# Layer 2's weight maxima first, its quantisation over 37 heads, and layer 1's maxima beside it through one raw buffer

## The chip, the cores and the metric

The kernel runs on one core of one Trainium2 chip. The metric is the device time of one launch in microseconds (us), the median of several runs. A core has five engines with their own instruction streams: TensorE (PE, matmul; its weight loads are listed apart as PEld), VectorE (DVE), ScalarE (ACT), GpSimd (POOL) and SyncE (SP), which here issues every DMA in one queue. They are tied by semaphores alone; nothing reorders the streams.

## The reference, cut to what matters

```python
x = x + tanh(g_xattn[0]) * L0_xattn_ref(ctx_2048, ctx_2048, layernorm(x), ssm_kernel, D, 8)   # x: (8, 512, 1024)
x = x + tanh(g_ffn[0]) * L0_ffn_ref(layernorm(x), ln_w, ln_b, W1, b1, W2, b2)

# the mixer, for each of 64 heads of 8 channels, over length L = 1024
kv = einsum('bhil,bhjl->bijhl', k, v)                  # here k = v, so kv is symmetric in i, j
y = irfft(rfft(kv, 2 * L) * rfft(ssm_kernel, 2 * L))[..., :L]
out = einsum('bijhl,bhil->bjhl', y + kv * D, q)

# the MLP: 1024 -> 4096 -> 1024, every operand in shared-exponent int8 blocks of 32
def mx_quant(x):
    amax = max(abs(x)) over blocks of 32
    scale = exp2(floor(log2(amax)) - 6)
    return clip(round(x / scale), -128, 127) * scale
h = mx_linear(mx_layernorm(x), W1, b1); h = mx_gelu(h); h = mx_linear(h, W2, b2)
```

## The kernel before, in words

The program has two stages. The first, `mixer_block`, does the convolution as matmuls with a Toeplitz slab of the taps, head by head, 64 heads in all. The second, `ffn_block`, does the MLP. Both weight matrices have to be quantised, which needs the maximum of each block of 32, and DVE does much of this beside the convolution, where PE is the busy engine.

A head `h` on PE is 78 matmuls in five stretches (L304 to L322). Its first stretch waits for `lo_ready`, the low half of the products kk of this head, which DVE makes at L495 in the head before. Its third stretch waits for `products_ready`, that is for DVE to have read the second half of the last head's result out of `y_ps`. In odd heads PE also transposes: `turn_back` (L343) after the first stretch and `turn_q` after the third.

DVE's order in head `h` is written out at L666 to L700. It starts when PE has finished head `h-1`:

1. `times_q(h-1, 1)`: L509, L512, L515 read the second half of the last head's result.
2. `make_kk(h+1)`: L486, L489. ACT then copies k, squares it and makes `kk_hi` (L395).
3. In even heads `ln_stats`, in odd heads `residual` (L658).
4. `times_q(h, 0)`, which waits for PE's second stretch of head `h`.
5. `low_half(h+1)`: L495, which waits for `kk_hi` and releases PE's head `h+1`.
6. What the texts below call the **filler** of head `h`: work for the MLP. It runs ahead of `times_q(h, 1)` in DVE's stream, so what of it is not done when PE starts head `h+1` delays step 1 of head `h+1`. That overhang is called the **carry** into head `h+1`.

The filler before the change: heads 0 to 19 hold 13 of the 32 tiles of weight maxima (L615, 1 MB each), and heads 3 to 20 also the norm and quantisation of the first input tiles. Heads 21 to 33 hold the other 19 maxima, two in each odd head and one in each even head except head 33. Head 34 makes all the scales (`weight_scales`, L640 to L648). Heads 35 to 63 hold layer 2's quantisation: 16 tiles of three instructions each, `layer2_ints` (L624), `layer2_clip` (L629), `layer2_quant` (L634). The maxima come through three raw buffers in `arena`, so that a load is issued two or three maxima ahead of its use.

SP's order in head `h` (L260 to L288): wait until PE has finished head `h-1` and issue two slab loads for head `h+1`; wait for `kk_ready` and `squares_ready` and load k for head `h+3`; in odd heads wait for `x1_ready`, store the x1 tile (L238) and load an x tile (L197); then loads of raw weights (L214 for maxima, L221 for quantisation) and stores of quantised ones (L226).

After the scales, layer 1's inverse scales are spread to all partitions in four steps at `spread_heads` (36, 38, 40, 42): ACT `repeat_inverses` (L421), PE `spread_inverses` (eight matmuls in the head's second stretch), ACT `keep_inverses` (L429). `turn_back` of the next odd head writes the same PSUM tile, so it waits for `inv_kept`. ACT's stream has `ln_apply` (L409, L413), which waits for POOL's `inv_sqrt` (L735), ahead of `keep_inverses`. POOL sums the products of each head (L748 to L760).

Of the kernel before, what the change touches and what calls it, by code (L numbers as in the profile page):

```python
# [20 lines left out]
L = 1024  # L21
HID = 4096
# [48 lines left out]
def mixer_block(nc, x_t, ctx_e, taps_in, skip_in, g_x, scratch, x1_t, w_m, w2_t, w2_q, ln_w, ln_b, arena, w_inv, rs, shift1,  # L71
# [10 lines left out]
    heads = tiles * TILE_HEADS  # L82
    row = LB * PAIR
    early_heads = 4 * EARLY
    maxima_heads = list(range(6)) + list(range(7, early_heads + 5, 2))
    maxima_heads += [early_heads + 5 + 2 * n // 3 for n in range(2 * W_TILES - len(maxima_heads))]
    maxima_of = [[n for n in range(2 * W_TILES) if maxima_heads[n] == h] for h in range(heads)]
    scales_head = maxima_heads[-1] + 1
    maxima_slot = [n % 2 if n < 12 else (n - 12) % 3 for n in range(2 * W_TILES)]
    spread_heads = [scales_head + 2 + scales_head % 2 + 2 * i for i in range(4)]  # L90
    w2_heads = heads - scales_head - 1
    ints_of, clip_of, quant_of = [{scales_head + 1 + (3 * j + i) * w2_heads // (3 * W_TILES): j for j in range(W_TILES)}
                                  for i in range(3)]
    y_base = -PARTS[0][0] * PAIR % 512
    edges = [0] + list(range(512 - y_base, row, 512)) + [row]
# [1 line left out]
    with ExitStack() as stack:  # L97
        def sb(name, shape, dt):
            return stack.enter_context(nc.sbuf_tensor(name, shape, dt))
# [4 lines left out]
        def sem(name):  # L104
            return stack.enter_context(nc.semaphore(name))
# [29 lines left out]
        w2_scale = w_max[:, 0:L // 2].bitcast(BF16)  # L135
        inv_rows = w_max[:, L:L + L // 2].bitcast(BF16)
        inv_T = raw_weights(arena, 1).bitcast(BF16)
        w_raw = w2_raw = [raw_weights(arena, i) for i in (2, 3, 0)]
        x1_last = raw_weights(arena, 2)[:, L:2 * L]
        w2_int = arena[:, X_LOADS * L:(X_LOADS + 1) * L].bitcast(I16)  # L140
        ident_bf = sb("ident_bf", [P, P], BF16)
# [21 lines left out]
        w_loaded = [sem(f"w_m_loaded{i}") for i in range(3)]  # L163
        w_max_ready, w_floor, w_bits, w_inv_ready = sem("w_max_ready"), sem("w_floor"), sem("w_bits"), sem("w_inv_ready")
# [26 lines left out]
        def _(sp):  # L191
# [15 lines left out]
            def load_w(n):  # L207
                slot = maxima_slot[n]
                users = [m for m in range(n) if maxima_slot[m] == slot]
                if users:  # L210
                    sp.wait_ge(w_max_ready, users[-1] + 1)
                elif slot == 2:
                    sp.wait_ge(e_input, EARLY)
                sp.dma_start(w_raw[slot], w_m[n]).then_inc(w_loaded[slot], 16)  # L214

            def load_w2(j):
                if j < 3:
                    sp.wait_ge(w_max_ready, 2 * W_TILES)
# [34 lines left out]
            load_k(2)  # L253
            for t in range(2, X_SLOTS):
                load_x(t)
            load_w(0)
            load_w(1)
            for dst, src in ((lnw_b, ln_w), (lnb_b, ln_b)):
                sp.dma_start(dst, bass.AP(tensor=src.tensor, offset=0, ap=[[0, P], [1, L]])).then_inc(ln_loaded, 16)
            for h in range(heads):  # L260
                t = h // TILE_HEADS
                if 1 <= h < heads - 1:
                    sp.wait_ge(y_ready, 2 * h)
                    load_slab(h + 1)
                if h + 3 < heads:
                    sp.wait_ge(kk_ready, h + 2)
                    sp.wait_ge(squares_ready, h + 2)
                    load_k(h + 3)
                if h % TILE_HEADS == 1 and t >= 1:
# [5 lines left out]
                if h == early_heads + 4:  # L275
                    load_w(14)
                for n in maxima_of[h - 1] if h >= 1 else []:
                    for m in range(n + 1, 2 * W_TILES):
                        if maxima_slot[m] == maxima_slot[n]:
                            load_w(m)  # L280
                            break
# [91 lines left out]
        def _(act):  # L373
# [41 lines left out]
                                     scale=rstd[:]).then_inc(xn_ready, 1)  # L415

            def repeat_inverses(r):
                act.wait_ge(w_inv_ready, 2)
                if r >= 1:
                    act.wait_ge(inv_spread, r)  # L420
                nc.scalar.copy(inv_rows.rearrange("p (n r k) -> p n r k", r=P // QB, k=QB),  # L421
                               view(w_inv, r * LB * QB, [(QB, LB), (0, P // QB), (1, QB)])).then_inc(inv_repeated, 1)

            def keep_inverses(r):
                if r == 0:
                    for turned in e_turned:
                        act.wait_ge(turned, 16 * EARLY // 2)
# [37 lines left out]
        def _(dve):  # L465
# [146 lines left out]
            def weight_maxima(n):  # L612
                nb = HID // 2 // QB
                dve.wait_ge(w_loaded[maxima_slot[n]], 16 * maxima_slot[:n + 1].count(maxima_slot[n]))
                nc.vector.tensor_reduce(w_max[:, n * nb:(n + 1) * nb], w_raw[maxima_slot[n]].rearrange("p (k i) -> p k i", k=nb),  # L615
                                        AX.X, ALU.max, apply_absolute_value=True).then_inc(w_max_ready, 1)

            def layer2_ints(j):
                dve.wait_ge(w2_loaded[j % 3], 16 * (j // 3 + 1))
                if j == 0:  # L620
                    dve.wait_ge(w_inv_ready, 2)
# [16 lines left out]
            def weight_scales():  # L638
                dve.wait_ge(w_max_ready, 2 * W_TILES)
                nc.vector.tensor_scalar(w_max[:], w_max[:], TINY, None, ALU.max).then_inc(w_floor, 1)  # L640
                dve.wait_ge(w_floor, 1)
                upper_half = w_max[:].bitcast(U16).rearrange("p (n two) -> p n two", two=2)[:, :, 1]
                nc.vector.tensor_scalar(w_inv.bitcast(U16), upper_half, EXP_BITS, EXP_BITS,
                                        ALU.bitwise_and, ALU.bitwise_xor).then_inc(w_bits, 1)
                dve.wait_ge(w_bits, 1)
                nc.vector.tensor_scalar(w_inv, w_inv, float(QB), None, ALU.mult).then_inc(w_inv_ready, 1)
                dve.wait_ge(w_inv_ready, 1)
                nc.vector.tensor_scalar(w2_scale.bitcast(U16), w_inv[:, L:2 * L].bitcast(U16), -1.0, 254.0 * 128,  # L648
                                        ALU.mult, ALU.add).then_inc(w_inv_ready, 1)

            def residual(t):
                dve.wait_ge(back_ready, t + 1)
# [13 lines left out]
            for h in range(heads):  # L666
# [700 lines left out]
```

## Time and profile before

| what | value |
|---|---|
| median of 3 runs | 1983.67 us (1983.58, 1983.67, 1988.19) |
| the profiled execution's own time | 1986.38 us |
| its span, first to last instruction | 1984.5 us |
| PE busy | 1899.7 us, 96% |
| DVE busy | 1694.7 us, 85% |
| POOL busy | 956.1 us, 48%; all of it in the first half |
| ACT busy | 755.0 us, 38% |
| the convolution on PE | its first matmul waits 17.7 us for the slab; it ends near 1019 us; 64 heads |
| mean granted PE clock | 0.984 of full speed |

An engine's busy share is a mean over stages. In the convolution the question is whether PE goes without a gap; where it does, time that DVE, ACT, POOL or a DMA spends costs nothing. In a timeline row a bracket at the end holds the engine's idle time before the row and what ended it.

### The profile page before, as it was taken

What the parts mean: (1) busy time and instruction counts of PE and PEld (TensorE: products, weight loads), DVE (VectorE), ACT (ScalarE), POOL (GpSimd) and SP (SyncE); (2) the same over time, 40 slices, a digit from 0 to 9 for tenths busy, and PEclk for the clock granted to TensorE, in tenths of its full rate; (3) what the DMA queues carried; (4) which work ended last, traced back from release to release, by engine and by line L of the source; (5) the groups of instructions that cost most, each with busy time, mean ns of one, the idle gap of its engine ahead of it and who ended that gap; (6) DMA issues with size and microseconds to landing.
All of it is one profiled execution on the core that took longest, in us unless ns stands there. A gap on an engine that the chain in (4) does not pass through costs nothing. (4 is left out here: it accounts for less than half of the span.)

```text
span 1984.5 us, 29456 instructions
## 1 busy us (share of the span) xinstructions
PE 1899.7 (96%) x11632; PEld 1498.6 (76%) x11680; DVE 1694.7 (85%) x2082; ACT 755.0 (38%) x1036; POOL 956.1 (48%) x1028
## 2 busy tenths in 40 slices
PE   6999999999999999999966997999999999999998
PEld 5988888888888898888954764666777666666773
DVE  6899999998897889898879798998888888898843
ACT  4333333333333433333303641444455444444440
POOL 4888899888898999999950000000000000000000
PEclk9999999999999999999978998999999999999999
DMA  6544446566644554555448412212222111221112
GB/s 247 192 174 157 157 153 205 207 229 216 222 172 153 192 190 166 194 181 193 143 162 336 150 43 75 67 62 64 75 75 75 65 54 64 75 67 51 54 43 75
DMA packets 99274, 271.75 MB, mean 137 GB/s; under 512 B 41472, under 2 KB 41472, under 8 KB 90944
## 3 DMA queue, kind: packets, MB, share of 16 engines
q1 hardware_dynamic: 99136, 269.86, 39.8%
q8 instruction: 92, 1.51, 0.3%
q14 instruction: 46, 0.38, 0.1%
HBM read 218.91 MB, written 42.53 MB: 132 GB/s over the span
## 5 line engine op out<-in xcount | busy, mean ns | idle before, releaser
L318 PE MATMUL y_ps<-kk_hi,slab 128*128 128x352 f32 (+6 forms) x3328 | 896.2, 351 | 21.0 <-DMA slab<-taps_scratch 17.7
L318 PEld LDWEIGHTS y_ps<-kk_hi,slab 128*128 128x128 f32 x3328 | 595.5, 189 | 90.1 <-issue 21.8
L318 PE MATMUL y_ps<-kk_lo,slab 128*128 128x512 f32 (+6 forms) x1664 | 581.0, 349 | 0.0
L976 PE MATMUL acc_ps<-w_T,arena 128*128 128x512 bf16 x2000 | 439.5, 379 | 2.5
L961 PE MATMUL l_ps<-f_xq_T,w_T 128*128 128x256 bf16 x3584 | 397.8, 274 | 15.6 <-ACT arena L1022 10.9
L961 PEld LDWEIGHTS l_ps<-f_xq_T,w_T 128*128 128x128 bf16 x3584 | 352.4, 98 | 61.9 <-ACT arena L1022 11.5
L976 PEld LDWEIGHTS acc_ps<-w_T,arena 128*128 128x128 bf16 x2048 | 200.4, 98 | 238.4
L1271 POOL TENSOR_TENSOR f_rstd<-f_var_eps,f_neg_half 128x1 f32<-128x1 f32 x28 | 15.3, 547 | 698.3 <-DVE f_var_eps L1081 698.3
L318 PEld LDWEIGHTS y_ps<-kk_lo,slab 128*128 128x128 f32 x1664 | 314.4, 189 | 34.4
L1022 ACT ACTIVATE arena<-l_ps,f_b 128x256 bf16<-128x256 f32 x512 | 213.2, 473 | 252.5 <-PE l_ps L961 247.4
L509 DVE TENSOR_TENSOR upper<-y_ps,q_ext 128x768 f32<-128x768 f32 (+1 forms) x128 | 155.9, 1218 | 97.1 <-PE y_ps L318 91.5
L748 POOL TENSOR_TENSOR lsum<-lower 128x240 f32<-128x240 f32 x127 | 169.0, 1331 | 65.9 <-DVE lower L515 65.8
L749 POOL TENSOR_TENSOR upper<-upper 128x384 f32<-128x384 f32 x127 | 183.5, 1445 | 0.0
L381 ACT COPY k_ps<-k_ext 128x512 f32<-128x512 f32 x64 | 37.9, 592 | 381.7 <-DVE kk L489 378.8
L495 DVE TENSOR_TENSOR kk_lo<-kk,kk_hi 128x2304 fp32r<-128x2304 f32 x64 | 172.1, 2689 | 6.1 <-ACT kk_hi L395 5.9
L760 POOL TENSOR_TENSOR mixed<-upper 128x192 f32<-128x192 f32 x127 | 158.4, 1247 | 18.5 <-POOL upper L757 0.4
L395 ACT CAST kk_hi<-kk 128x2304 fp32r<-128x2304 f32 x64 | 136.2, 2128 | 9.6 <-DVE kk L489 7.6
L1029 ACT ACTIVATE arena<-arena 128x2048 bf16<-128x2048 bf16 x64 | 121.9, 1910 | 0.5
L515 DVE TENSOR_TENSOR lower<-y_ps,q_ext 128x576 f32<-128x576 f32 (+1 forms) x128 | 121.1, 946 | 0.0
L751 POOL TENSOR_TENSOR lsum<-lsum,lower 128x240 f32<-128x240 f32 x127 | 119.1, 938 | 0.0
L1001 ACT ACTIVATE f_n<-arena,f_shift,f_rstd 128x1024 bf16<-128x1024 f32 x28 | 34.5, 1240 | 213.6 <-POOL f_shift L1273 213.6
L486 DVE TENSOR_TENSOR kk<-k_ps,k_ext 128x1536 f32<-128x1536 f32 x64 | 111.7, 1746 | 1.2 <-ACT k_ps L381 1.2
(135 smaller groups left out, 2061.9 us busy)
## 6 DMA issues: line engine op xcount, KB each, us to landing
slab<-taps_scratch SPq DMA_DIRECT2D x128, 512.0 KB, 4.8
arena<-in_w_m SPq DMA_DIRECT2D x32, 1024.0 KB, 6.4
arena<-x_scratch SPq DMA_DIRECT2D x60, 512.0 KB, 3.8
k_ext<-in_ctx_e SPq DMA_DIRECT2D x64, 384.0 KB, 3.5
arena<-in_w SPq DMA_DIRECT2D x18, 1024.0 KB, 6.9
x_tile<-in_x_t SPq DMA_DIRECT2D x32, 512.0 KB, 6.2
out_t<-arena SPq DMA_DIRECT2D x32, 512.0 KB, 2.6
x_scratch<-x SPq DMA_DIRECT2D x31, 512.0 KB, 4.5
```

The source lines that it names most:

```text
L318: mm = nc.tensor.matmul(y_ps[:, y_base + begin:y_base + end], slab[s][:, half, d * P:(d + 1) * P], kk_part[s][:, begin - d * PAIR:end - d ...
L395: nc.scalar.copy(kk_hi[h % 2][:], kk[:].rearrange("p n c -> p (n c)")).then_inc(hi_ready, 1)
L495: nc.vector.tensor_tensor(kk_lo[h % 2][:], kk[:].rearrange("p n c -> p (n c)"), kk_hi[h % 2][:].bitcast(F32), ALU.subtract).then_inc(lo_re ...
L509: nc.vector.tensor_tensor(view(up, 0, [((DIAG + 1) * CH, count), (CH, DIAG), (1, CH)]), view(y_ps, y_at, [(PAIR, count), (CH, DIAG), (1, C ...
L515: nc.vector.tensor_tensor(view(low, B, [(3 * ACCW, count), (ACCW + B, 3), (1, CH)]), view(y_ps, y_at + CH, [(PAIR, count), (CH, 3), (1, CH)]),
L748: add(lsum[:, :, B:], low[:, :, 0, B:], low[:, :, 1, B:], ALU.add).then_inc(lower_two, 1)
L749: add(up[:, :, 0:2, :], up[:, :, 0:2, :], up[:, :, 2:4, :], ALU.add).then_inc(upper_two, 1)
L760: add(out, rows[0], rows[4], ALU.add).then_inc(sums_ready, 1)
L961: mm = nc.tensor.matmul(l1_ps[bank % L1_BANKS][:, a, :], w1_T[:, b, k, a * P:(a + 1) * P], inputs[:, k, :], start=(k == 0), stop=(k == L / ...
L976: mm = nc.tensor.matmul(acc_ps[s][:, c * 512:(c + 1) * 512], hidden[g % 2][:, k, s * P:(s + 1) * P], w2_T[:, k, c * 512:(c + 1) * 512], st ...
L1022: done = nc.scalar.activation(hidden[g % 2][:, c, :], l1_ps[bank % L1_BANKS][:, a, :], ACT.Identity, bias=b1_c[:, c:c + 1])
L1029: nc.scalar.activation(h, h, ACT.Gelu_apprx_tanh).then_inc(gelu_ready, 1)
```

## The change

The order of DVE's filler is recast, with SP's loads to match. Layer 2's 16 tiles of maxima come first (heads 0 to 5, then the odd heads 7 to 25). Head 26 makes layer 2's scales (`layer2_scales`). From head 27 on two things run beside each other: layer 2's quantisation, whose 48 instructions are now spread over 37 heads (27 to 63), and layer 1's 16 tiles of maxima, in heads 27, 28, 30, 31, 33, 34 and so on to 48, 49, two in each three heads. Head 50 makes layer 1's scales, and `spread_heads` become 52, 54, 56, 58.

Since the quantisation has the raw buffers 2, 3 and 0, layer 1's maxima get one raw buffer of their own, number 1, and `load_maxima1(n)` waits for maxima `n-1` to have been read. SP issues it one head behind maxima `n-1`. Layer 2's maxima use two buffers. The wait on the early transposes moves from ACT's `keep_inverses` to SP's `load_maxima1(0)`. DVE gets three instructions more, since the scales are made in two parts; the bytes moved are the same.

```diff
-    maxima_heads = list(range(6)) + list(range(7, early_heads + 5, 2))
-    maxima_heads += [early_heads + 5 + 2 * n // 3 for n in range(2 * W_TILES - len(maxima_heads))]
-    scales_head = maxima_heads[-1] + 1
-    maxima_slot = [n % 2 if n < 12 else (n - 12) % 3 for n in range(2 * W_TILES)]
-    spread_heads = [scales_head + 2 + scales_head % 2 + 2 * i for i in range(4)]
-    w2_heads = heads - scales_head - 1
-    ints_of, clip_of, quant_of = [{scales_head + 1 + (3 * j + i) * w2_heads // (3 * W_TILES): j for j in range(W_TILES)}
+    maxima2_heads = list(range(6)) + list(range(7, early_heads + 11, 2))
+    scales2_head = maxima2_heads[-1] + 1
+    maxima1_heads = [scales2_head + 1 + 3 * n // 2 for n in range(W_TILES)]
+    scales1_head = maxima1_heads[-1] + 1
+    spread_heads = [scales1_head + 2 + scales1_head % 2 + 2 * i for i in range(4)]
+    w2_heads = heads - scales2_head - 1
+    ints_of, clip_of, quant_of = [{scales2_head + 1 + (3 * j + i) * w2_heads // (3 * W_TILES): j for j in range(W_TILES)}
...
-        w_raw = w2_raw = [raw_weights(arena, i) for i in (2, 3, 0)]
+        w2_raw, w1_raw = [raw_weights(arena, i) for i in (2, 3, 0)], raw_weights(arena, 1)
...
+            def load_maxima1(n):
+                if n == 0:
                     sp.wait_ge(e_input, EARLY)
-                sp.dma_start(w_raw[slot], w_m[n]).then_inc(w_loaded[slot], 16)
+                    for turned in e_turned:
+                        sp.wait_ge(turned, 16 * EARLY // 2)
+                else:
+                    sp.wait_ge(max1_ready, n)
+                sp.dma_start(w1_raw, w_m[n]).then_inc(maxima1_loaded, 16)
...
-                if h == maxima_heads[-1] + 1:
+                if h - 1 in maxima2_heads and maxima2_heads.index(h - 1) + 2 < W_TILES:
+                    load_maxima2(maxima2_heads.index(h - 1) + 2)
+                if h == scales2_head:
+                    load_maxima1(0)
                     for j in range(3):
                         load_w2(j)
+                if h - 1 in maxima1_heads and maxima1_heads.index(h - 1) + 1 < W_TILES:
+                    load_maxima1(maxima1_heads.index(h - 1) + 1)
...
+            def layer1_maxima(n):
+                nb = HID // 2 // QB
+                dve.wait_ge(maxima1_loaded, 16 * (n + 1))
+                nc.vector.tensor_reduce(w_max[:, n * nb:(n + 1) * nb], w1_raw.rearrange("p (k i) -> p k i", k=nb),
+                                        AX.X, ALU.max, apply_absolute_value=True).then_inc(max1_ready, 1)
...
-                for n in maxima_of[h]:
-                    weight_maxima(n)
-                if h == scales_head:
-                    weight_scales()
+                if h in maxima2_heads:
+                    layer2_maxima(maxima2_heads.index(h))
+                if h in maxima1_heads:
+                    layer1_maxima(maxima1_heads.index(h))
+                if h == scales2_head:
+                    layer2_scales()
+                if h == scales1_head:
+                    layer1_scales()
```

DVE's stream at head 31, a head in which layer 1's maxima tile follows that of the head before. `kk_lo` releases PE's head 32, and `upper` of 5x256 is the start of `times_q(31, 1)`. Before, with two maxima tiles as filler:

```order
L495 TENSOR_TENSOR kk_lo<-kk,kk_hi 128x2304
L615 TENSOR_REDUCE w_max<-arena 128x64 x2
L509 TENSOR_TENSOR upper<-y_ps,q_ext 128x5x256
L512 TENSOR_TENSOR upper<-y_ps,q_ext 128x5x64
L515 TENSOR_TENSOR lower<-y_ps,q_ext 128x5x3x64
L486 TENSOR_TENSOR kk<-k_ps,k_ext 128x8x192
```

Of the change, at the same place:

```order
L497 TENSOR_TENSOR kk_lo<-kk,kk_hi 128x2304
L623 TENSOR_REDUCE w_max<-arena 128x64
L632 TENSOR_TENSOR arena<-arena,b_b 128x2048
L511 TENSOR_TENSOR upper<-y_ps,q_ext 128x5x256
L514 TENSOR_TENSOR upper<-y_ps,q_ext 128x5x64
L517 TENSOR_TENSOR lower<-y_ps,q_ext 128x5x3x64
L488 TENSOR_TENSOR kk<-k_ps,k_ext 128x8x192
```

One maxima tile and one `layer2_ints` (L632) stand where two maxima tiles stood.

SP's queue in heads 30 and 31 (each head begins with the two slab loads; `in_w_m` are the weights for maxima, `in_w` those for quantisation). Before:

```order
L205 DMA slab<-taps_scratch 128x1024 x2
L200 DMA k_ext<-in_ctx_e 128x768
L214 DMA arena<-in_w_m 128x2048 x2
L205 DMA slab<-taps_scratch 128x1024 x2
L200 DMA k_ext<-in_ctx_e 128x768
L238 DMA x_scratch<-x_0 128x1024
L197 DMA x_tile<-in_x_t 128x1024
L214 DMA arena<-in_w_m 128x2048
```

Of the change:

```order
L205 DMA slab<-taps_scratch 128x1024 x2
L200 DMA k_ext<-in_ctx_e 128x768
L228 DMA arena<-in_w 128x2048
L205 DMA slab<-taps_scratch 128x1024 x2
L200 DMA k_ext<-in_ctx_e 128x768
L245 DMA x_scratch<-x_0 128x1024
L197 DMA x_tile<-in_x_t 128x1024
L219 DMA arena<-in_w_m 128x2048
L233 DMA w_scratch<-arena 128x2048
```

The load at L219 in head 31 is that of the very maxima tile which DVE reads at L623 in head 31; before, the loads of head 31 and its neighbours were for maxima in later heads.

## Rows read from the trace of the kernel before

**Rows 1.** Windows: us, busy of each engine (instructions), clock, DMA share, GB/s

```profile
561.70:567.10 5.40, 5.40 (x37) 5.39 (x36) 5.30 (x5) 0.24 (x1) 5.40 (x5) 1.00 0.99 397
598.40:601.70 3.30, 0.29 (x3) 0.06 (x1) 3.30 (x4) 3.20 (x3) 3.30 (x6) 0.87 0.27 109
601.70:607.70 6.00, 5.97 (x18) 5.07 (x19) 2.15 (x3) 3.26 (x3) 5.86 (x7) 0.50 0.48 147
700.00:800.00 100.00, 100.00 (x554) 89.22 (x553) 89.27 (x89) 35.85 (x39) 97.57 (x93) 1.00 0.52 177
```

**Rows 2.** Waits of PE from 100 to 1020 us: total, times, longest

```profile
PE y_ps L318 <- issue: 3.4, 7, 1.0
```

**Rows 3.** Timeline of DVE in head 22: start, duration, instruction

```profile
362.56 4.47 DVE L615 TENSOR_REDUCE w_max<-arena 128x64 f32<-128x2048 f32 x2
...
375.38 2.67 DVE L495 TENSOR_TENSOR kk_lo<-kk,kk_hi 128x2304 fp32r<-128x2304 f32 x1
```

**Rows 4.** Timeline of PE at the start of head 23

```profile
378.15 0.40 PE L318 MATMUL y_ps<-kk_hi,slab 128*128 128x352 f32 x1 [0.60 <-issue]
```

**Rows 5.** Timeline of SP's queue, heads 29 to 31 (start, issue time)

```profile
470.95 0.80 SPq L205 DMA_DIRECT2D slab<-taps_scratch  x2
...
478.75 1.32 SPq L214 DMA_DIRECT2D arena<-in_w_m  x1
487.25 0.80 SPq L205 DMA_DIRECT2D slab<-taps_scratch  x2
...
495.43 0.90 SPq L214 DMA_DIRECT2D arena<-in_w_m  x2
501.81 0.80 SPq L205 DMA_DIRECT2D slab<-taps_scratch  x2
```

**Rows 6.** Timeline of DVE, heads 29 and 30

```profile
475.70 0.41 DVE L489 TENSOR_TENSOR kk<-k_ps,k_ext 128x256 f32<-128x256 f32 x1
...
484.40 4.47 DVE L615 TENSOR_REDUCE w_max<-arena 128x64 f32<-128x2048 f32 x2
...
493.32 0.41 DVE L489 TENSOR_TENSOR kk<-k_ps,k_ext 128x256 f32<-128x256 f32 x1
...
499.84 2.28 DVE L615 TENSOR_REDUCE w_max<-arena 128x64 f32<-128x2048 f32 x1
```

**Rows 7.** Line L214, one load each: heads 29 and 31 (odd), head 30 (even)

```profile
L214 SPq DMA_DIRECT2D arena<-in_w_m x1: 1322/1322/1322, 478.7 to 478.7; - x1
DMA to landing us min/median/max: 7.7/7.7/7.7
...
L214 SPq DMA_DIRECT2D arena<-in_w_m x1: 1280/1280/1280, 509.6 to 509.6; - x1
DMA to landing us min/median/max: 8.4/8.4/8.4
...
L214 SPq DMA_DIRECT2D arena<-in_w_m x1: 423/423/423, 495.4 to 495.4; - x1
DMA to landing us min/median/max: 5.3/5.3/5.3
```

**Rows 8.** Groups by line and form, DVE: busy us, mean ns, idle before

```profile
L615 DVE TENSOR_REDUCE w_max<-arena 128x64 f32<-128x2048 f32 x32 | 72.4, 2276 | 0.0
L624 DVE TENSOR_TENSOR arena<-arena,b_b 128x2048 int16<-128x2048 f32 x16 | 43.4, 2710 | 0.6
...
L634 DVE TENSOR_TENSOR arena<-arena,w_max 128x2048 bf16<-128x2048 int16 x16 | 26.4, 1651 | 0.2
...
L629 DVE TENSOR_SCALAR arena<-arena 128x2048 int16<-128x2048 int16 x16 | 18.8, 1173 | 0.2
```

**Rows 9.** Timelines of ACT and PE at head 37

```profile
598.21 0.29 ACT L409 ACTIVATE shift<-neg_mean,rstd 128x1 f32<-128x1 f32 x1 [7.80 <-POOL rstd L735]
...
600.61 1.02 ACT L429 CAST arena<-turn_ps 128x1024 bf16<-128x1024 f32 x1
...
601.73 1.94 PE L353 MATMUL turn_ps<-ident,mixed 128*128 128x128 f32 x8 [3.04 <-issue]
```

More of the change, by code:

```diff
@@ L134, in mixer_block @@
         w_max = sb("w_max", [P, HID // 2], F32)
-        w2_scale = w_max[:, 0:L // 2].bitcast(BF16)
-        inv_rows = w_max[:, L:L + L // 2].bitcast(BF16)
+        w2_scale = w_max[:, L:L + L // 2].bitcast(BF16)
+        inv_rows = w_max[:, L + L // 2:2 * L].bitcast(BF16)
         inv_T = raw_weights(arena, 1).bitcast(BF16)
-        w_raw = w2_raw = [raw_weights(arena, i) for i in (2, 3, 0)]
+        w2_raw, w1_raw = [raw_weights(arena, i) for i in (2, 3, 0)], raw_weights(arena, 1)
         x1_last = raw_weights(arena, 2)[:, L:2 * L]
@@ L162, in mixer_block @@
         k_loaded = [sem("k_loaded0"), sem("k_loaded1")]
-        w_loaded = [sem(f"w_m_loaded{i}") for i in range(3)]
-        w_max_ready, w_floor, w_bits, w_inv_ready = sem("w_max_ready"), sem("w_floor"), sem("w_bits"), sem("w_inv_ready")
+        maxima2_loaded, maxima1_loaded = [sem("w2_m_loaded0"), sem("w2_m_loaded1")], sem("w1_m_loaded")
+        max2_ready, max1_ready, w_floor, w_bits, inv2_ready, inv1_ready = (
+            sem(n) for n in ("w2_max_ready", "w1_max_ready", "w_floor", "w_bits", "w2_inv_ready", "w1_inv_ready"))
         w2_ints, w2_clipped, w2_quant = sem("w2_ints"), sem("w2_clipped"), sem("w2_quant")
@@ L205, in load_slab, with load_maxima2 @@
                     sp.dma_start(slab[h % 2][:, half, :].bitcast(F32), src).then_inc(slab_loaded[h % 2], 16)
[L207 to L212, printed above, removed]
-                    sp.wait_ge(e_input, EARLY)
-                sp.dma_start(w_raw[slot], w_m[n]).then_inc(w_loaded[slot], 16)
+            def load_maxima2(n):
+                if n >= 2:
+                    sp.wait_ge(max2_ready, n - 1)
+                sp.dma_start(w2_raw[n % 2], w_m[W_TILES + n]).then_inc(maxima2_loaded[n % 2], 16)
+            def load_maxima1(n):
+                if n == 0:
+                    sp.wait_ge(e_input, EARLY)
+                    for turned in e_turned:
[3 more added lines that the diff above has]
+                sp.dma_start(w1_raw, w_m[n]).then_inc(maxima1_loaded, 16)
             def load_w2(j):
-                if j < 3:
-                    sp.wait_ge(w_max_ready, 2 * W_TILES)
+                if j < 2:
+                    sp.wait_ge(max2_ready, W_TILES - 1 + j)
+                elif j == 2:
+                    sp.wait_ge(e_input, EARLY)
                 else:
@@ L255, in _ @@
                 load_x(t)
-            load_w(0)
-            load_w(1)
+            load_maxima2(0)
+            load_maxima2(1)
             for dst, src in ((lnw_b, ln_w), (lnb_b, ln_b)):
@@ L274, in _ @@
                     turn_early((h - 9) // 4)
[L275 to L281, printed above, removed]
-                if h == maxima_heads[-1] + 1:
+                if h - 1 in maxima2_heads and maxima2_heads.index(h - 1) + 2 < W_TILES:
+                    load_maxima2(maxima2_heads.index(h - 1) + 2)
+                if h == scales2_head:
+                    load_maxima1(0)
                     for j in range(3):
                         load_w2(j)
+                if h - 1 in maxima1_heads and maxima1_heads.index(h - 1) + 1 < W_TILES:
+                    load_maxima1(maxima1_heads.index(h - 1) + 1)
                 if h - 2 in quant_of and quant_of[h - 2] + 3 < W_TILES:
@@ L417, in repeat_inverses @@
             def repeat_inverses(r):
-                act.wait_ge(w_inv_ready, 2)
+                act.wait_ge(inv1_ready, 1)
                 if r >= 1:
@@ L424, in keep_inverses @@
             def keep_inverses(r):
-                if r == 0:
-                    for turned in e_turned:
-                        act.wait_ge(turned, 16 * EARLY // 2)
                 act.wait_ge(inv_spread, r + 1)
@@ L610, in early_quantise, with layer2_maxima @@
                 nc.vector.tensor_tensor(grid, grid, view(scale_x, 0, [(0, QB), (1, nb1)]), ALU.mult).then_inc(x_quant, 1)
-            def weight_maxima(n):
+            def layer2_maxima(n):
                 nb = HID // 2 // QB
-                dve.wait_ge(w_loaded[maxima_slot[n]], 16 * maxima_slot[:n + 1].count(maxima_slot[n]))
-                nc.vector.tensor_reduce(w_max[:, n * nb:(n + 1) * nb], w_raw[maxima_slot[n]].rearrange("p (k i) -> p k i", k=nb),
-                                        AX.X, ALU.max, apply_absolute_value=True).then_inc(w_max_ready, 1)
+                dve.wait_ge(maxima2_loaded[n % 2], 16 * (n // 2 + 1))
+                nc.vector.tensor_reduce(w_max[:, L + n * nb:L + (n + 1) * nb], w2_raw[n % 2].rearrange("p (k i) -> p k i", k=nb),
+                                        AX.X, ALU.max, apply_absolute_value=True).then_inc(max2_ready, 1)
+            def layer1_maxima(n):
[3 more added lines that the diff above has]
+                                        AX.X, ALU.max, apply_absolute_value=True).then_inc(max1_ready, 1)
             def layer2_ints(j):
@@ L620, in layer2_ints @@
                 if j == 0:
-                    dve.wait_ge(w_inv_ready, 2)
+                    dve.wait_ge(inv2_ready, 2)
                 else:
@@ L636, in layer2_quant, with weight_inverses, layer2_scales, layer1_scales @@
                                         w2_scale_twice, ALU.mult).then_inc(w2_quant, 1)
[L638 to L643, printed above, removed]
-                                        ALU.bitwise_and, ALU.bitwise_xor).then_inc(w_bits, 1)
-                dve.wait_ge(w_bits, 1)
-                nc.vector.tensor_scalar(w_inv, w_inv, float(QB), None, ALU.mult).then_inc(w_inv_ready, 1)
-                dve.wait_ge(w_inv_ready, 1)
+            def weight_inverses(layer, n):
+                maxima = w_max[:, layer * L:(layer + 1) * L]
+                inverse = w_inv[:, layer * L:(layer + 1) * L]
+                nc.vector.tensor_scalar(maxima, maxima, TINY, None, ALU.max).then_inc(w_floor, 1)
+                dve.wait_ge(w_floor, n)
+                upper_half = maxima.bitcast(U16).rearrange("p (n two) -> p n two", two=2)[:, :, 1]
+                nc.vector.tensor_scalar(inverse.bitcast(U16), upper_half, EXP_BITS, EXP_BITS,
+                                        ALU.bitwise_and, ALU.bitwise_xor).then_inc(w_bits, 1)
+                dve.wait_ge(w_bits, n)
+                return nc.vector.tensor_scalar(inverse, inverse, float(QB), None, ALU.mult)
+            def layer2_scales():
+                dve.wait_ge(max2_ready, W_TILES)
+                weight_inverses(1, 1).then_inc(inv2_ready, 1)
+                dve.wait_ge(inv2_ready, 1)
                 nc.vector.tensor_scalar(w2_scale.bitcast(U16), w_inv[:, L:2 * L].bitcast(U16), -1.0, 254.0 * 128,
-                                        ALU.mult, ALU.add).then_inc(w_inv_ready, 1)
+                                        ALU.mult, ALU.add).then_inc(inv2_ready, 1)
+            def layer1_scales():
+                dve.wait_ge(max1_ready, W_TILES)
+                weight_inverses(0, 2).then_inc(inv1_ready, 1)
             def residual(t):
```

1 line of the change is left out of this document (removed).

## The prediction

> **What bounds the kernel now.** I read three views in this order. First the windows by stage. From 700 to 800 us PE is busy for all 100 us, and DVE for 89 [rows 1]. So in the convolution PE sets the time, and DVE's filler is free as long as `kk_lo` comes before PE needs it. The change touches only this stage, so the question is where PE waits, before and after.
>
> Second, the list of PE's waits from 100 to 1020 us. At the convolution's matmuls they come to 3.4 us in 7 places, the longest 1.0 us [rows 2]. One more, of 3.04 us, stands before `turn_back` in head 37 [rows 9]. That is all there is to gain by ordering filler better: the limit of a gain is small before any working.
>
> Third, the timelines, from which I take the rule of a head. SP issues the slab loads as soon as PE has ended a head, so the rows of L205 give the beats: 470.95, 487.25, 501.81 [rows 5]. An odd head lasts 16.3 us and an even one 14.6. In head 22 DVE's filler of head 21 ends at 362.56 + 4.47 = 367.0, and `kk_lo` of the next head ends at 375.38 + 2.67 = 378.05, which is 11.05 us later [rows 3]. PE starts head 23 at 378.15, after 0.60 us of idle [rows 4]. So with carry F into a head, `kk_lo` ends at F + 11.05, and the head is late when F is over 16.3 - 11.15 = 5.15 (odd) or 14.6 - 11.15 = 3.45 (even). With a small carry `kk_lo` waits for PE instead, and filler begins before the head's end: at 484.40 against 487.1, so 2.7 us, in an odd head, and at 499.84 against 501.65, so 1.8 us, in an even head [rows 5, 6].
>
> **The change part by part.**
>
> *Filler durations.* Mean ns: maxima 2276, ints 2710, clip 1173, quant 1651 [rows 8]. Instructions back to back overlap by 0.08 us (two maxima take 4.47 [rows 3]), so I use 2.2, 2.65, 1.1 and 1.6. The work in total is what it was, and DVE has room on average: what matters is one head at a time.
>
> *Heads 20 to 25* lose a maxima tile each. The wait of 0.60 us before head 23 [rows 4] goes: DVE's filler of head 21 is halved. Gain 0.6.
>
> *The wait at head 37.* ACT waits for POOL until 598.21, then does `ln_apply` and `keep_inverses`, which ends at 600.61 + 1.02 = 601.63; PE starts `turn_back` at 601.73 [rows 9]. PE's clock is 0.50 from 601.7 to 607.7 [rows 1], where 5.97 us of matmul would have taken 3. Together 3.0 + 3.0 = 6.0 us. The spread moves to head 52, so this goes from head 37. Gain 6.0; what comes back at head 53 is priced below.
>
> *The one raw buffer.* This is the cost. Maxima tiles stand in pairs of heads: 27, 28, then 30, 31 and so on. The second of a pair is loaded by SP in the very head in which DVE reads it, for the buffer is free only once the first has been read, and SP gets to it after k's load. SP comes to that load 1.7 us after `make_kk` in an even head (495.43 against 493.32 + 0.41) and 2.65 us after it in an odd head, behind the x1 store and the x load (478.75 against 475.70 + 0.41) [rows 5, 6]. `make_kk` ends at F + 4.85 (493.73 against 484.40 + 4.47 [rows 6]). The load then takes 5.3 us in an even head and 7.7 or 8.4 in an odd one [rows 7]; I take 8.0. So the tile is there at F + 11.85 in even heads and at F + 15.5 in odd ones. DVE wants it when `kk_lo` is done, at F + 11.05, or 13.6 in an odd head with small carry. The even second heads (28, 34, 40, 46) cost DVE 0.8 us at most. The odd ones (31, 37, 43, 49) cost 3.5 to 4.5 us of DVE standing still with `times_q` queued behind it, and PE's next head behind that. The Trainium skill's page DMA: Bandwidth & Descriptors (section Bandwidth) gives 6.15 us for 1 MB. By it each odd wait would be 1.85 us shorter and the sum below some 6 lower, by estimate. The rows have the same transfer at 7.7 and 8.4 in this place, so the sum goes by them.
>
> Head by head, for those that come out late:
>
> - Head 31. Head 30's filler is 2.2 + 1.1 + 1.6 = 4.9, so F = 4.9 - 1.8 = 3.1. The tile lands at 18.6. Then 2.2 + 2.65: the filler ends at 23.5, and the carry is 23.5 - 16.3 = 7.2. Head 32 is late by 7.2 - 3.45 = 3.75.
> - Head 37. Head 36 holds 2.2 + 2.65, so F = 3.1; lands at 18.6; then 2.2 + 1.1 + 1.6; carry 7.2; head 38 late by 3.75.
> - Head 43. F = 2.2 + 1.6 - 1.8 = 2.0; lands at 17.5; then 2.2 + 2.65 + 1.1; carry 7.2; head 44 late by 3.75.
> - Head 49. F = 2.2 + 1.1 - 1.8 = 1.5; lands at 17.0; then 2.2 + 1.6; carry 4.5; head 50 late by 1.05.
> - Head 50 holds the scales (before, the four of them filled 5.3 us [rows 1]; the three for one layer, at half size, about 2.4) with ints and clip: 6.15. `kk_lo` ends at 15.55, PE's head at 15.65, so the carry is 6.05, and head 51 late by 0.9.
> - Head 33's filler, 2.2 + 1.6 + 2.65 = 6.45, gives F = 3.8 and head 34 late by 0.35. Head 27's 5.95 just fits.
>
> Sum 13.55.
>
> *Head 53.* `turn_back` waits there as at 37. The carry into 52 is about 1.5, and the quantisation, which before ran at 16 tiles in 29 heads, now runs at 16 in 37. So POOL's sums should come earlier than at 37. Bounds 0 and 6.0; I take 1, nearer to the low end, since before only the first of four such places waited.
>
> *PE's clock.* Each head that is late by 3.75 us has two idle pieces: about 1.8 before its third stretch (`times_q` ends at F + 2.9 = 10.1, PE is there at 8.3) and 2.0 before the next head. After the idle of up to 1.0 us [rows 2] the clock is still at 1.00 in the windows, and after that of 3.04 us it was 0.50 for 6 us and cost 3.0 [rows 1, 9]. Two us lies between. Three such heads: bounds 0 and 9; I take 2.
>
> *DVE instructions added* (three, under 1 us each) lie in that filler and are counted. *The four 1 MB loads in head 26* are one more than before in head 34, where DMA ran at 397 GB/s [rows 1]; 4 MB at that rate is 10.5 us, and the slabs of head 28 are wanted a whole head later. Nothing.
>
> Net: 13.55 + 1 + 2 - 0.6 - 6.0 = +9.95 us. On the profiled execution's own 1986.38 us that is 1996.3; it stands 2.7 above the median of 1983.67, from which I get **1993.6 us**.
>
> **The rivals.** 0.3% (6 us) is about what a measurement of this kernel can tell from no change.
>
> - A, *short landings.* In odd heads the load lands after 5.3 us as in even ones, since SP's other transfers are nearly done. Each odd wait is 2.7 us shorter. Heads 32, 38 and 44 are late by 1.05 each, 50 not, 51 by 0.35: sum 3.85, the clock stays up, net 3.85 + 1 - 6.6 = -1.75, so 1981.9. For it: the 5.3. Against it: 7.7 and 8.4 with the very same rows ahead.
> - B, *the clock falls and head 53 waits in full.* 13.55 + 6 + 9 - 6.6 = +21.95, so 2005.6. For it: both happened at head 37. Against it: POOL has less to wait out, and the new idle comes in pieces.
> - C, the other side, *no wait for the buffer at all.* SP's load would have to be there when `kk_lo` ends in head 31, at 3.1 + 11.05 = 14.15; it is issued at 10.6, so it would have to land in 3.6 us; with 4.3 PE would still not notice. Then only 0.35 and 0.9 remain, head 53 takes nothing, and the net is 1.25 - 6.6 = -5.35, so 1978.3, at the edge of 0.3%. No row has a megabyte in under 5.3 us here.
>
> **How the numbers follow.** Chances: as forecast 0.60, A 0.18, B 0.14, C 0.08. The forecast's own band, with landings of 7.7 to 8.4 and the clock at 0 to 6, is 1989 to 1999. The range has to reach past A and most of the way to B: 1980 to 2003. Faster by over 0.3% (under 1977.7) holds the part of C in which something small comes on top: 0.06. Within 0.3% (to 1989.6): A, the rest of C, and the low end of the forecast: 0.30. Slower: 0.64.
>
> **What would show it.** In the trace after, DVE should wait for a DMA at the maxima line for layer 1, four times 3.5 to 4.5 us and some times under 1. PE should show idle of about 2 us before the third stretch of heads 32, 38 and 44 and again before the head after. The wait at `turn_back` in head 37 should be gone, and that in head 53 under 2 us. The clock should be near 0.98 on the mean again. The prediction is wrong if the loads in odd heads land within 5 us, if SP issues them much earlier than 10 us into the head, or if POOL, not DVE, holds up `times_q`.

## The result, and the profile after

| | median | span of the profiled execution |
|---|---|---|
| before, runs beside the changed kernel | 1985.35 us (1983.58 to 1988.19, 4 runs) | 1984.5 us |
| after | 2001.70 us (2001.18 to 2002.79, 4 runs) | 2000.4 us |

The ratio is 1.0076, with a 95% interval of 1.0063 to 1.0089. So the change makes the kernel slower, by 16.35 us between the medians where 9.95 were forecast.

First the page of the kernel after, its busy times:

```profile
PE 1907.9 (95%) x11680; PEld 1502.0 (75%) x11680; DVE 1693.9 (85%) x2085; ACT 754.9 (38%) x1036; POOL 952.0 (48%) x1028
```

DVE's busy time is what it was, 1694 us. No work was added that matters; the time is in waits. (PE's busy time is 8 us higher than before; 5 us of this are 48 matmuls of the MLP, L976, whose records the profile of the kernel before lacks. PE's instructions are the same in both.) The list of PE's waits from 100 to 1032 us, after:

```profile
PE y_ps L323 <- issue: 10.7, 12, 1.7
PE y_ps L323 <- DVE lower L517: 4.9, 4, 2.0
PE turn_ps L358 <- issue: 2.2, 1, 2.2
```

PE stood still for 3.4 us in 7 places at the convolution's matmuls [rows 2]; now it is 10.7 + 4.9 = 15.6 us in 16 places. The single wait at `turn_back` is smaller, 2.2 us for 3.04 [rows 9], and has moved to head 53. The waits of DVE for a DMA, and the group with what they stand at (columns as in rows 8):

```profile
L623 DVE TENSOR_REDUCE w_max<-arena 128x64 f32<-128x2048 f32 x16 | 36.5, 2279 | 20.3 <-DMA arena<-in_w_m 20.3
```

In [rows 8] the same instruction had 0.0 us of idle ahead of it. Now DVE waits 20.3 us for layer 1's tiles. One of these waits in full, head 31, from three timelines of the kernel after. SP's queue:

```profile
502.80 0.80 SPq L205 DMA_DIRECT2D slab<-taps_scratch  x2
512.53 0.33 SPq L200 DMA_DIRECT2D k_ext<-in_ctx_e  x1
512.91 0.43 SPq L245 DMA_DIRECT2D x_scratch<-x  x1
513.38 0.43 SPq L197 DMA_DIRECT2D x_tile<-in_x_t  x1
513.86 1.30 SPq L219 DMA_DIRECT2D arena<-in_w_m  x1
```

The landing of that load (line L219, this one issue):

```profile
L219 SPq DMA_DIRECT2D arena<-in_w_m x1: 1296/1296/1296, 513.9 to 513.9; - x1
...
DMA to landing us min/median/max: 8.1/8.1/8.1
```

DVE:

```profile
514.70 2.70 DVE L497 TENSOR_TENSOR kk_lo<-kk,kk_hi 128x2304 fp32r<-128x2304 f32 x1 [0.58 <-ACT kk_hi L400]
522.00 2.29 DVE L623 TENSOR_REDUCE w_max<-arena 128x64 f32<-128x2048 f32 x1 [4.60 <-DMA arena<-in_w_m]
524.20 2.28 DVE L632 TENSOR_TENSOR arena<-arena,b_b 128x2048 int16<-128x2048 f32 x1
526.40 1.48 DVE L511 TENSOR_TENSOR upper<-y_ps,q_ext 128x1280 f32<-128x1280 f32 x1
```

And PE, in head 32 and at the start of head 33:

```profile
529.40 0.50 PE L323 MATMUL y_ps<-kk_hi,slab 128*128 128x512 f32 x1 [2.01 <-DVE lower L517]
...
537.63 0.40 PE L323 MATMUL y_ps<-kk_hi,slab 128*128 128x352 f32 x1 [1.73 <-issue]
```

The reader sees the chain in one piece. The load is issued at 513.86 and lands 8.1 us later, at 522.0. DVE had ended `kk_lo` at 517.4 and does nothing for 4.6 us. Its filler ends at 526.4, when `times_q` can begin, but PE started head 32 at 518.9. So PE waits 2.0 us for `times_q`, and at the end of the head 1.7 us more for `kk_lo`, which in this trace ends at 537.5.

Length of the heads that differ from 14.57 us (even, 15.07 in a spread head) or 16.3 us (odd), read from each head's first matmul in the timelines; only heads 21 to 62:

| head | before | after | later than nominal, after | forecast |
|---|---|---|---|---|
| 22 | 15.33 | 14.57 | 0 | 0 |
| 32 | 14.57 | 18.72 | 4.15 | 3.75 |
| 34 | 14.57 | 15.33 | 0.76 | 0.35 |
| 37 | 22.29 | 16.30 | 0 | 0 |
| 38 | 15.07 | 17.68 | 3.11 | 3.75 |
| 39 | 16.30 | 17.88 | 1.58 (clock) | clock, 2 in all |
| 44 | 14.57 | 18.17 | 3.60 | 3.75 |
| 50 | 14.57 | 16.09 | 1.52 | 1.05 |
| 51 | 16.30 | 18.01 | 1.71 | 0.9 |
| 53 | 16.30 | 18.66 | 2.36 | 1 |

The new lateness is 18.8 us against 16.55 forecast, and 6.75 us went at heads 22 and 37 (6.6 forecast): +12.1 us in these heads.

### The profile page after: what moved, and what is told of

It is laid out like the page before. It is cut to its first block and busy times, and to the rows that moved or that the text cites. A ratio compares the mean times of both kernels' runs of the same rounds, so it can differ in the third digit from the quotient of the medians.

```text
span 2000.4 us, 29507 instructions
## 1 busy us (share of the span) xinstructions
PE 1907.9 (95%) x11680; PEld 1502.0 (75%) x11680; DVE 1693.9 (85%) x2085; ACT 754.9 (38%) x1036; POOL 952.0 (48%) x1028
## 5 line engine op out<-in xcount | busy, mean ns | idle before, releaser
L997 PE MATMUL acc_ps<-w_T,arena 128*128 128x512 bf16 x2048 | 444.5, 379 | 0.0
L982 PE MATMUL l_ps<-f_xq_T,w_T 128*128 128x256 bf16 x3584 | 399.4, 275 | 15.0 <-ACT arena L1043 10.3
L769 POOL TENSOR_TENSOR lsum<-lower 128x240 f32<-128x240 f32 x127 | 156.3, 1231 | 83.2 <-DVE lower L517 82.8
L781 POOL TENSOR_TENSOR mixed<-upper 128x192 f32<-128x192 f32 x127 | 152.0, 1197 | 18.5 <-POOL upper L778 0.4
L772 POOL TENSOR_TENSOR lsum<-lsum,lower 128x240 f32<-128x240 f32 x127 | 123.3, 971 | 0.0
```

The costliest lines, as they stand in the source:

```text
L769: add(lsum[:, :, B:], low[:, :, 0, B:], low[:, :, 1, B:], ALU.add).then_inc(lower_two, 1)
L772: add(lsum[:, :, B:], lsum[:, :, B:], low[:, :, 2, B:], ALU.add).then_inc(lower_all, 1)
L781: add(out, rows[0], rows[4], ALU.add).then_inc(sums_ready, 1)
L982: mm = nc.tensor.matmul(l1_ps[bank % L1_BANKS][:, a, :], w1_T[:, b, k, a * P:(a + 1) * P], inputs[:, k, :], start=(k == 0), stop=(k == L / ...
L997: mm = nc.tensor.matmul(acc_ps[s][:, c * 512:(c + 1) * 512], hidden[g % 2][:, k, s * P:(s + 1) * P], w2_T[:, k, c * 512:(c + 1) * 512], st ...
```

## The experiments

The kernel before had a median of 1987.44 us on the chip of the first four and 1987.03 us on that of the last three, where the table above has 1985.35. The changed kernel did not run on these chips. So a difference from its 2001.70 us mixes two chips, which alone can make 2 us; what a single head gains is read from the traces.

**1. The tile's load ahead of k's.** SP issues `load_maxima1` right behind the slab loads.

```diff
                     load_slab(h + 1)
+                if h - 1 in maxima1_heads and maxima1_heads.index(h - 1) + 1 < W_TILES:
+                    load_maxima1(maxima1_heads.index(h - 1) + 1)
...
-                if h - 1 in maxima1_heads and maxima1_heads.index(h - 1) + 1 < W_TILES:
-                    load_maxima1(maxima1_heads.index(h - 1) + 1)
```

> The changed kernel, but SP issues the load of layer 1's next maxima tile right behind the two slab loads of a head, ahead of the wait on kk_ready and k's load. Nothing moves on DVE. Theory (the tile of the second head of a pair lands too late, and DVE stands still for it with times_q queued behind): the waits of DVE for a DMA at the layer 1 maxima (20.3 us in 7 places after the change) fall under 2 us, heads 32, 38, 44, 50 are on time or late by under 1 us each, and the kernel gets 11 to 14 us faster than the changed one, about 1989. Rival (the filler of heads 27 to 50 is too dense for DVE, whatever the loads do): the wait moves to kk_lo, heads stay late, and at most 3 us come back, about 1999.

Measured: 1984.65 us (11 runs), ratio to before 0.9987 (0.9978 to 0.9996), and 17 us faster than the changed kernel, more than the 11 to 14 expected. The profile of DVE has no wait for a DMA at L623 any more. In head 31 the load goes out 0.9 us behind the slab loads instead of 11.1, and DVE goes on without a gap:

```profile
503.33 0.80 SPq L205 DMA_DIRECT2D slab<-taps_scratch  x2
504.19 0.42 SPq L219 DMA_DIRECT2D arena<-in_w_m  x1
512.98 0.33 SPq L200 DMA_DIRECT2D k_ext<-in_ctx_e  x1
```

```profile
515.16 2.68 DVE L497 TENSOR_TENSOR kk_lo<-kk,kk_hi 128x2304 fp32r<-128x2304 f32 x1 [0.58 <-ACT kk_hi L400]
517.75 2.28 DVE L623 TENSOR_REDUCE w_max<-arena 128x64 f32<-128x2048 f32 x1
519.95 2.40 DVE L632 TENSOR_TENSOR arena<-arena,b_b 128x2048 int16<-128x2048 f32 x1
```

The load itself did not get faster: it lands 7.7 us after this issue. It is issued so early that this no longer matters. Heads 32, 38, 39, 44, 50 and 51 have their nominal lengths, head 34 is 0.2 us late. The rival, that DVE's filler is too dense in heads 27 to 50, falls: the same filler in the same heads costs 0.2 us. PE's waits over the convolution, of this kernel:

```profile
PE y_ps L323 <- issue: 2.8, 6, 1.0
PE turn_ps L358 <- issue: 1.8, 1, 1.8
```

**2. The tile's load ahead of the x1 store only.**

```diff
+                if h - 1 in maxima1_heads and maxima1_heads.index(h - 1) + 1 < W_TILES:
+                    load_maxima1(maxima1_heads.index(h - 1) + 1)
                 if h % TILE_HEADS == 1 and t >= 1:
                     store_x1(t - 1)
```

> The changed kernel, but in odd heads SP issues the load of the maxima tile ahead of the x1 store and the x tile load instead of behind them; still behind k's load. Theory: an odd second head then behaves as an even one, the tile is issued some 1 us earlier and lands 5.3 us instead of about 8 after that, so each of the four long waits shrinks by 3 to 3.5 us; heads 32, 38 and 44 are late by about 0.5 each, and 9 to 11 us come back, about 1991. Rival (the place in the queue does not matter, only bandwidth that all four transfers share): the landing stays near 8 us, 1 us per wait comes back, about 1998.

Measured: 1992.61 us (7 runs), ratio 1.0030 (1.0019 to 1.0041): by the medians 9.1 us of the loss came back, at the low end of what was expected, and by the lengths of heads 32 to 51 7.7 us. DVE's waits at L623 are 9.8 us instead of 20.3. Head 31 in this kernel, SP, the landing and DVE:

```profile
512.38 0.33 SPq L200 DMA_DIRECT2D k_ext<-in_ctx_e  x1
512.76 0.43 SPq L219 DMA_DIRECT2D arena<-in_w_m  x1
513.23 0.43 SPq L245 DMA_DIRECT2D x_scratch<-x  x1
```

```profile
DMA to landing us min/median/max: 6.4/6.4/6.4
```

```profile
519.15 2.29 DVE L623 TENSOR_REDUCE w_max<-arena 128x64 f32<-128x2048 f32 x1 [1.91 <-DMA arena<-in_w_m]
```

1.1 us of the gain is the earlier issue and 1.7 us the shorter landing, 6.4 for 8.1. Half of the latter is SP's own time: as the fourth DMA in a row this issue took 1.30 us, here it takes 0.43. The landing is not the 5.3 us of an even head that was expected; the x1 and x transfers are now issued right behind it, and that they take a share of the DMA engines is argued, not shown. So heads 32, 38 and 44 stay late by 1.6, 1.9 and 0.75 us, and the clock falls twice, in heads 33 and 39, for 1.6 and 1.5 us.

**3. `keep_inverses` ahead of `ln_apply`.**

```diff
+                if h in spread_heads:
+                    keep_inverses(spread_heads.index(h))
                 if t + 1 < tiles:
                     if h % TILE_HEADS == 0:
                         ln_apply(t + 1)
...
-                if h in spread_heads:
-                    keep_inverses(spread_heads.index(h))
```

> The changed kernel, but ACT does keep_inverses ahead of ln_apply in the four spread heads. Theory (turn_back waits in head 53 because keep_inverses stands behind ln_apply, which waits for POOL): the idle of 2.15 us before turn_back in head 53 goes and nothing takes its place; 2.2 to 2.4 us faster than the changed kernel, about 1999.3. Rival (the wait is for the spread itself or for POOL's sums): no difference, 2001.7.

Measured: 1999.45 us (5 runs), ratio 1.0065 (1.0051 to 1.0079), 2.25 us faster than the changed kernel, which the medians of two chips would not show alone. The trace does: head 53 lasts 16.3 us instead of 18.66. ACT in this kernel, in head 52 and the start of 53:

```profile
854.88 1.00 ACT L431 CAST arena<-turn_ps 128x1024 bf16<-128x1024 f32 x1
862.66 0.30 ACT L414 ACTIVATE shift<-neg_mean,rstd 128x1 f32<-128x1 f32 x1 [6.78 <-POOL rstd L756]
```

The copy that PE's `turn_back` needs is done 6.8 us before ACT gets what it waits for from POOL. In the changed kernel it stood behind that wait.

**4. The same edit in the kernel before.**

> The kernel before, with the same one edit: ACT does keep_inverses ahead of ln_apply in heads 36, 38, 40 and 42. Theory (the 3.04 us idle and the 6 us at the lower clock in head 37 both come from keep_inverses behind ln_apply): head 37 lasts 16.3 us instead of 22.3, and the kernel takes 6.0 us less than the kernel before, about 1979.4. Rival (the clock would have fallen for another reason, or turn_back waits for POOL's sums as well): 3 us or nothing.

Measured: 1982.77 us (11 runs), ratio to before 0.9978 (0.9969 to 0.9987): 4.7 us between the medians where 6.0 were expected; the interval reaches from 2.6 to 6.2 us. In the trace head 37 is 16.3 us long instead of 22.3, all of the 6.0, and the window that holds it is full, at full clock (columns as in rows 1):

```profile
590.00:620.00 30.00, 30.00 (x176) 27.07 (x175) 27.04 (x27) 12.47 (x14) 29.43 (x30) 1.00 0.47 149
```

Heads 21 and 22 got 0.55 us longer. Head 21 is some 0.45 us too long in all three kernels that have this edit and the old early maxima. There the carry into it is 5.6 us, over the limit of 5.15, where the kernel before has 5.09; small DVE instructions of the filler take longer (L600, 0.76 us for 0.16). Nothing moved there, and why they do stays open.

**5. Edits 1 and 3 together.**

> The changed kernel with both edits: the load of the maxima tile right behind the slab loads, and keep_inverses ahead of ln_apply. Theory (the two costs are apart and add): heads 27 to 63 all last 16.3 or 14.6 us (15.1 in the four spread heads), and it is 2 us faster than with the early load alone, about 1982.6. Rival (with head 53 on time, POOL or DVE holds up a head behind it): no gain over the early load alone.

Measured: 1982.21 us (7 runs), ratio 0.9972 (0.9961 to 0.9983), 2.4 us faster than edit 1 alone. The two intervals overlap, but the traces show the sum: head 53 lasts 16.3 us where experiment 1 has 18.3, and the heads that edit 1 mended stay mended. PE's waits over its convolution, of this kernel, are those of heads 9 to 21:

```profile
PE y_ps L323 <- issue: 3.0, 7, 1.0
```

**6. Edits 1 and 3, and layer 2's maxima out of heads 9 to 17.**

```diff
-    maxima2_heads = list(range(6)) + list(range(7, early_heads + 11, 2))
+    maxima2_heads = list(range(7)) + [19, 21, 22, 23, 23, 24, 24, 25, 25]
...
                     load_slab(h + 1)
+                for n in maxima2_of[h - 1] if h >= 1 else []:
+                    if n + 2 < W_TILES:
+                        load_maxima2(n + 2)
```

(The main lines; `...` stands for what lies between. The loads of layer 2's maxima too are now issued right behind the slab loads.)

> As the last one, and the maxima tiles of layer 2 leave heads 9, 11, 13, 15 and 17, where the early norm and quantisation stand beside them, for heads 6 and 22 to 25, with their loads too right behind the slabs. Theory (a head is late when its carry is over 3.45 or 5.15 us, and in heads 9 to 18 the tiles put it there): the lateness of 4.2 us in heads 9 to 18 goes (0.5, 0.35, 1.25, 0.35, 1.4, 0.35), about 1978.5. Rival (those heads are late for the early norm's own waits for POOL): under 1 us comes back, 1982.

Measured: 1978.89 us (5 runs), ratio 0.9960 (0.9947 to 0.9972), 3.3 us faster than the last. Of 4.25 us of lateness in heads 9 to 18, 0.9 is left; in the trace the carries into heads 13 and 17 fell from 6.4 us to 5.4, near the limit of 5.15. It was the tiles and not the earlier loads that did it: DVE waited for none of layer 2's loads before, either. The rival, waits of the early norm for POOL, falls.

```profile
PE y_ps L325 <- issue: 0.4, 2, 0.2
```

**7. The kernel before with edit 3, and its maxima out of heads 9 to 17.**

```diff
-    maxima_heads = list(range(6)) + list(range(7, early_heads + 5, 2))
-    maxima_heads += [early_heads + 5 + 2 * n // 3 for n in range(2 * W_TILES - len(maxima_heads))]
+    maxima_heads = list(range(6)) + [7, 19] + [early_heads + 5 + (n + 1) // 2 for n in range(2 * W_TILES - 8)]
...
-    maxima_slot = [n % 2 if n < 12 else (n - 12) % 3 for n in range(2 * W_TILES)]
+    maxima_slot = [n % 2 if n < 8 else (n - 8) % 3 for n in range(2 * W_TILES)]
...
                     load_slab(h + 1)
+                for n in maxima_of[h - 1] if h >= 1 else []:
+                    for m in range(n + 1, 2 * W_TILES):
+                        if maxima_slot[m] == maxima_slot[n]:
+                            load_w(m)
+                            break
```

(The main lines again. Here too the loads of the maxima are issued right behind the slab loads, and the edit of experiment 3 is in.)

> The kernel before with keep_inverses ahead of ln_apply, and its five maxima tiles of heads 9 to 17 moved into heads 22 to 32, two tiles a head from 22 to 32, loads right behind the slabs. Theory: heads 9 to 18 as in the run before, and the 0.75 us of head 22 goes or stays, 4 to 5 us faster than with keep_inverses alone, about 1978. If the changed kernel's new arrangement is worth something of its own, the run before is clearly faster than this one; if not, they are the same.

Measured: 1978.08 us (5 runs), ratio 0.9953 (0.9940 to 0.9967), 4.7 us faster than experiment 4. By its median this is the fastest version. PE has no gap left that counts:

```profile
100.00:1010.00 910.00, 909.47 (x5085) 815.14 (x5085) 828.74 (x850) 321.76 (x357) 850.11 (x863) 1.00 0.55 185
```

It beats experiment 6, on the same chip, by 0.8 us, which the runs (1976.55 to 1978.83 and 1978.23 to 1980.21) hardly tell apart. So no worth of its own shows for the new arrangement of the filler. Once no head is late, PE has next to no idle left in the convolution that an order of filler could remove.

## Why the prediction came out right, point by point

**The bound.** PE in the convolution, with DVE's filler free until a head's carry passes its limit: right, and shown by experiments 1 and 6, which leave DVE's work as it is and only remove waits or move tiles. The limits of 3.45 and 5.15 us hold closely. The carries into heads 32, 34, 38, 44 and 50 were 7.58, 4.18, 6.53, 7.03 and 4.95 us, which is 4.13, 0.73, 3.08, 3.58 and 1.50 over 3.45; these heads were late by 4.15, 0.76, 3.11, 3.60 and 1.52. Head 51 had 6.89, 1.74 over 5.15, and was late by 1.71.

**The one raw buffer.** The mechanism is shown by experiment 1. By its numbers for head 31: issue at 11.2 us into the head against 10.6 forecast, landing 8.1 us against 8.0, DVE's wait 4.6 us against "3.5 to 4.5"; the other three odd heads had 4.25, 4.4 and 3.7. The carry into heads 32, 38 and 44 was 7.6, 6.5 and 7.0 us against 7.2 each. One even head went past the forecast's "0.8 us at most": head 34 waited 2.0 us. Its load took 6.4 us to land where the sum had 5.3; a 512 KB store of quantised weights was issued right behind it, for which the sum had no term. PE did not feel it, since the next head is an odd one and its carry of 5.12 stayed within the limit. The Trainium skill's 6.15 us for 1 MB (DMA: Bandwidth & Descriptors, section Bandwidth) was too short for this place in the queue, where the trace has 8.1 us; with two transfers fewer ahead of it, in experiment 2, it is near, 6.4 us. The forecast's estimate from it was loose as well: by its own rule of the carry, four waits shorter by 1.85 us make the sum 7.4 us lower, not 6.

**Short heads of the sum.** Heads 34, 50 and 51 were 1.7 us later in all than forecast. For head 34 it is one instruction: its carry was 4.2 us against 3.8, and `layer2_quant` ahead of it took 1.92 us where the sum had 1.6. For the others a small error is carried on: the carry into head 49 was 2.8 us against 1.5, the tile landed at 17.8 us against 17.0, and the carry into head 50 was 4.95 against 4.5; then head 50's filler took 7.0 us against 6.15, so that head 51 got 6.9 against 6.05.

**Head 53.** Mis-sized: 2.36 us where I took 1. That it is `keep_inverses` behind `ln_apply` is shown by experiment 3. The forecast had POOL come much earlier than at head 37, since the quantisation is spread thinner. It came 0.9 us earlier: ACT got `rstd` at 2.5 us into head 53, and at 3.5 us into head 37 before. That DVE was late in heads 50 and 51, from which POOL takes its products, explains little of it: in experiment 1 both heads are on time, and `turn_back` still waits 1.8 us of the 2.2. What the trace has is two of POOL's additions in head 52, beside `kk_lo` (854.42 to 856.96) and `layer2_ints` (856.89 to 859.85) on DVE:

```profile
854.51 3.20 POOL L776 TENSOR_TENSOR upper<-upper,lsum 128x320 f32<-128x320 f32 x1
857.67 2.50 POOL L778 TENSOR_TENSOR upper<-upper,lsum 128x120 f32<-128x120 f32 x1
```

One head earlier, in head 51, the same two take 0.88 and 0.45 us. That is 4.4 us more, and the kernel before has the like in head 36 (2.77 us for 0.46, and `rstd` 2.60 us). That DVE's instructions beside them are the cause is argued; no run moves them.

**The clock.** Taken at 2 us; 1.58 in the trace, in head 39 alone. That size is one execution's: in experiment 3, with the same queue of loads, it fell in heads 33 and 45, for 1.6 us each. Windows of the kernel after, over heads 33 and 39:

```profile
537.20:543.20 6.00, 5.57 (x36) 5.48 (x37) 6.00 (x6) 2.67 (x2) 5.86 (x9) 1.00 0.93 381
633.80:640.20 6.40, 6.03 (x30) 6.06 (x31) 6.40 (x6) 2.62 (x2) 6.40 (x7) 0.73 0.77 305
```

The idle ahead of both was 1.7 us; the clock stayed up after the one and fell after the other.

**What goes.** 6.0 us at head 37, as forecast, and 0.76 at head 22 for the 0.6 forecast; experiment 4 shows the first in the kernel before.

**What lies between forecast and result.** The forecast was +9.95 us, the medians differ by 16.35. Of the 6.4 us between them 2.1 are the terms above. Another 3.5 us lie where nothing was moved: head 0 lasts 18.2 us instead of 16.8 in the two traces, and the MLP from the convolution's end on 967.4 instead of 965.4. The rest is a first matmul that starts 0.3 us later, and the medians, which differ by 0.4 us more than the two profiled executions.

Both of the larger pieces go with the clock. In the kernel before and in experiment 5, which have the shortest heads 0 (16.8 us), the granted clock rises at 20.6 and 20.8 us; in the three kernels with the longest (18.0 to 18.2 us) it rises at 23.6 to 24.4. In the MLP the clock is at 0.50 for 51.2 us in experiments 2 and 3 (MLP 965.3 and 964.9 us), for 54.6 us in the three kernels with the old arrangement (965.0 to 965.4), for 58.0 us in the changed kernel and experiments 1 and 5 (967.1 to 967.4), and for 61.4 us in experiment 6 (967.8). So an MLP of 965 us occurs with the new arrangement too, and the 2 us need not be the change; but 967 us and more occurs with it alone, and one profile for each kernel cannot tell the two apart. The spread also shows in the medians: the kernel before has 1987.4 us on one other chip, 3.8 above the median that the prediction started from. Experiment 1 against the changed kernel, 17 us, has 16.7 us of it in heads 1 to 63.

So the size came out low, by two fifths, and past the forecast's own band; that it stayed inside the full range owes something to how wide that was, for rival B. The path of the loss, its heads and its cause are as forecast.

**The rivals.** A (short landings) is refuted by the 8.1 us, B by the clock, which fell once of three times, and by head 53, which lost 2.4 us and not 6, and C by the 20.3 us. Two of their prices had a slip: without a wait in head 49 the forecast's own rule gives a carry of 12.85 + 6.15 - 14.6 = 4.4 us into head 51, under 5.15, so that head is on time. A kept 0.35 us for it and C 0.9, and C should have read 1977.4 us. Experiment 1 bears this out: a carry of 4.99 us and no lateness. The forecast's own band was 1989 to 1999; the median is 2.7 above it, for the reasons given above.

## What to carry to other kernels

When filler is spread beside a busy engine, look at each slot's length and not at the mean: here DVE had room in total before and after, and what cost 16 us was a load of one megabyte that went out some 10 us later in its head than it could have, and four long waits for it. A single buffer that is used in two neighbouring slots needs its reload issued at the first point at which it is free, ahead of anything in the queue that waits for something else. And where an in-order engine has two duties in one slot, the one that another engine waits for goes first, if the other may itself wait: that single exchange gave 4.7 us in the kernel before, more than the whole new arrangement of the filler, which by experiments 6 and 7 gives nothing that shows.

## What the runs showed of the hardware

- The same 1 MB load from HBM, from the start of its issue, landed in 5.1 to 5.7 us behind k's load alone (changed kernel, heads 28, 32, 40, 44 and 46), in 6.3 and 6.4 us with a 512 KB store right behind it (heads 34 and 38), in 6.3 to 6.9 us with two 512 KB transfers right behind it (experiment 2, odd heads), and in 7.5 to 10.3 us with the same two ahead of it (changed kernel, odd heads). Right behind the two slab loads it took 6.9 to 8.6 us (experiment 1).
- SP's issue of this load took 0.44 us or less in second place behind k's load, and 1.25 to 1.34 us in fourth place (changed kernel).
- PE's clock went from 2.4 to 1.2 GHz (granted 1.00 to 0.50) after idle pieces well under the 3.04 us of [rows 9]. In experiment 2 one idle of 1.45 us was followed by 3.4 us at the lower clock, and the head after it was 1.6 us longer than nominal. After 2.0 and 1.7 us around head 32 of the changed kernel it stayed up, and after 1.0 and 1.7 us at the same place in experiment 3 it fell. What decides between them these runs leave open.
- The clock first rises between 20.6 and 24.4 us of the span. Counted from PE's first matmul it is 2.9 us in the kernel before and 6.1 us in the changed one, and head 0 is 1.4 us longer in the latter.
- Two POOL additions of 0.88 and 0.45 us took 3.20 and 2.50 us where DVE ran `kk_lo` and `layer2_ints` beside them (changed kernel, head 52).
